# Moving the split of the normalised tokens into two bf16 halves from VectorE to GpSimd, in a layer kernel on eight cores

## The reference

```python
x = L0_attn_x                       # (8, 2048, 1024)
xn = _layernorm(x, axis=-1)         # (x - mean) / sqrt(var + 1e-5)
x = x + _L0_attn_ref(xn, ...) + _L0_ffn_ref(xn, ...)

# attention: holo_linear(x, basis, phase, amp):
resonance = jnp.einsum('bli,hi->blh', x, basis)     # 1024 -> 32
w = amp * jnp.cos(phase)
return jnp.einsum('blh,oh->blo', resonance, w)      # 32 -> 1024
# ffn:
logits = x.astype(jnp.float32) @ gate_w.astype(jnp.float32).T
topk_w, topk_i = jax.lax.top_k(softmax(logits), 2)
g = silu(einsum('td,edf->etf', x, w_gate)) * einsum('td,edf->etf', x, w_up)
expert_out = einsum('etf,efd->etd', g, w_down)
```

## Time and profile before

| what | value |
|---|---|
| time, median of 2 runs | 3964.53 us (3963.12 to 3965.94) |
| the profiled execution | 3961.37 us |
| its span, first to last instruction | 3959.8 us |
| spans of the 8 cores | 3954.5 to 3959.8 us |
| mean granted TensorE clock | 0.923 on the profiled core |

### The profile page before, as it was taken

How to read it: one execution, slowest core, us unless ns; L and a number is a source line. 1 busy time by engine, 2 the same in 40 slices (tenths; PEclk the granted TensorE clock), 3 DMA queues, 4 the chain that set the end, 5 groups by cost and what they waited for, 6 DMA issues and landing times.

```text
span 3959.8 us, 45402 instructions; the slowest of 8 cores (3954.5 to 3959.8 us)
## 1 busy us (share of the span) xinstructions
PE 3079.4 (78%) x13795; PEld 1211.7 (31%) x13795; DVE 1821.3 (46%) x2660; ACT 870.2 (22%) x945; POOL 267.5 (7%) x351
## 2 busy tenths in 40 slices
PE   2444355555554489999999999999999999999996
PEld 1111011111111034343443333434334343344432
DVE  4444534444444444444444555544444455433344
ACT  0222166666664011111111100111111110011100
POOL 1000000000000101100000000111000000011000
PEclk9755599999998599999999999999999999999995
DMA  1000000000000143343333333334433333334205
GB/s 30 27 27 17 0 0 1 1 1 1 1 1 11 19 46 38 37 48 39 33 33 33 33 33 33 35 36 48 44 33 33 33 33 33 33 39 48 27 1 160
DMA packets 254434, 116.01 MB, mean 29 GB/s; under 512 B 233592, under 2 KB 233592, under 8 KB 254208
## 3 DMA queue, kind: packets, MB, share of 16 engines
q0 software_dynamic: 245248, 87.87, 21.5%
q1 hardware_dynamic: 8960, 25.24, 2.1%
HBM read 191.40 MB, written 8.39 MB: 50 GB/s over the span
## 4 chain that ended last, share of the span: by engine, by line
PE 67%; ACT 14%; DVE 10%; issue 6%; DMA 2%; DVEq 1%; POOL 0%; ACTq 0%; SPq 0%; POOLq 0%
PE p_xg L817 20%; PE p_xu L826 19%; PE p_d L859 19%; ACT pTs L636 13%; PE p_st L625 4%; PE p_t L411 2%; DVE acc L867 1%; DMA out<-o 1%; PE p_pj L295 1%; DVE gbuf L841 1%; DVE acc L718 1%; DVE o_heads L680 1%; PE p_a L606 1%; DMA wdbuf<-w_down 1%; DVE o L910 1%
## 5 line engine op out<-in xcount | busy, mean ns | idle before, releaser
L859 PE MATMUL p_d<-gbuf,wdbuf 128*128 128x512 bf16 x3520 | 836.3, 377 | 63.3 <-DVE acc L867 35.1
L817 PE MATMUL p_xg<-xnh_fm,wgbuf 128*128 128x512 bf16 x3520 | 843.7, 383 | 25.7 <-DMA wdbuf<-w_down 25.7
L826 PE MATMUL p_xu<-xnh_fm,wubuf 128*128 128x512 bf16 x3520 | 833.8, 380 | 0.0
L841 DVE TENSOR_TENSOR gbuf<-sgt,p_xu 128x512 bf16<-128x512 bf16 x440 | 302.7, 688 | 978.0 <-PE p_xu L826 947.7
L836 ACT ACTIVATE sgt<-p_xg 128x512 bf16<-128x512 f32 x440 | 262.8, 597 | 2175.6 <-PE p_xg L817 1582.8
L867 DVE TENSOR_TENSOR acc<-acc,p_d 128x512 f32<-128x512 f32 x896 | 615.5, 687 | 259.4 <-PE p_d L859 244.0
L636 ACT ACTIVATE pTs<-p_st,bias 128x2048 bf16<-128x2048 f32 x256 | 503.6, 1967 | 337.7 <-PE p_st L625 328.1
L817 PEld LDWEIGHTS p_xg<-xnh_fm,wgbuf 128*128 128x128 bf16 x3520 | 346.3, 99 | 450.0 <-issue 42.1
L826 PEld LDWEIGHTS p_xu<-xnh_fm,wubuf 128*128 128x128 bf16 x3520 | 345.4, 98 | 418.7 <-issue 6.1
L859 PEld LDWEIGHTS p_d<-gbuf,wdbuf 128*128 128x128 bf16 x3520 | 284.5, 96 | 610.6 <-issue 391.2
L625 PE MATMUL p_st<-q_fm,k_fm 64*128 64x512 bf16 x1024 | 162.3, 392 | 311.6 <-ACT pTs L636 311.2
(11 more groups left out here) (200 smaller groups left out, 1024.4 us busy)
## 6 DMA issues: line engine op xcount, KB each, us to landing
wgbuf<-w_gate POOLq DMA_DIRECT2D x88, 256.0 KB, 14.0
wubuf<-w_up POOLq DMA_DIRECT2D x88, 256.0 KB, 15.0
wdbuf<-w_down POOLq DMA_DIRECT2D x88, 256.0 KB, 16.0
x_tm<-x SPq DMA_DIRECT2D x16, 512.0 KB, 3.5
x<-x SPq DMA_DIRECT2D x16, 512.0 KB, 4.5
out<-o SPq DMA_DIRECT2D x16, 512.0 KB, 5.1
wgbuf<-sw_gate POOLq DMA_DIRECT2D x22, 256.0 KB, 11.1
wubuf<-sw_up POOLq DMA_DIRECT2D x22, 256.0 KB, 11.7
```

The source lines that it names most:

```text
L817: emit("tensor", lambda te, buf=buf, loc=loc, c=c, tg=tg, pb=pg_b: te.matmul(pb[:, :], wgbuf[buf][:, loc * 1024 + c * 128: loc * 1024 + c ...
L826: emit("tensor", lambda te, buf=buf, loc=loc, c=c, tg=tg, pb=pu_b: te.matmul(pb[:, :], wubuf[buf][:, loc * 1024 + c * 128: loc * 1024 + c ...
L841: emit("vector", lambda v, gs=gslice, ss=ss, pb=pu_b: v.tensor_tensor(gs, sgt[ss][:], pb[:, :], ALU.mult), waits=[("t", t_xu), ("s", s_sil ...
L859: first=(li == 0), last=(li == len(grp) - 1): te.matmul(pb[:, :], wdbuf[buf][:, li * 1024 + dc * 128: li * 1024 + dc * 128 + 128], gbuf[bu ...
```

## The change

The cast and the subtraction that split `xn_tm` into its halves are put into POOL's list in place of DVE's. The cast waits for DVE's scaling and, as before, for the old transposes; the subtraction waits for POOL's semaphore after the cast. All 16 transposes of a tile wait for POOL's count after the subtraction. The subtraction of the mean, which writes `xn_tm`, now also waits until POOL has read the previous tile from it.

```diff
@@ -376,7 +377,7 @@
              incs=[("v", 1)])
         emit("vector", lambda v, b=b: v.tensor_single_scalar(
             xn_tm[:], x_tm[b][:], m_t[:], ALU.subtract),
-            waits=[("s", s_sq_prev)], incs=[("v", 1)])
+            waits=[("s", s_sq_prev), ("g", g_hl_prev)], incs=[("v", 1)])
...
         hb = i % 2
-        emit("vector", lambda v, hb=hb: v.tensor_copy(xnh_tm[hb][:], xn_tm[:]),
-             waits=[hilo_free[hb]], incs=[("v", 1)])
-        emit("vector", lambda v, hb=hb: v.tensor_tensor(
-            xnl_tm[hb][:], xn_tm[:], xnh_tm[hb][:], ALU.subtract), incs=[("v", 1)])
-        v_hl = cnt["v"]
+        v_xn_ready = cnt["v"]
+        emit("gpsimd", lambda g, hb=hb: g.tensor_copy(xnh_tm[hb][:], xn_tm[:]),
+             waits=[hilo_free[hb], ("v", v_xn_ready)], incs=[("g", 1)])
+        g_hi = cnt["g"]
+        emit("gpsimd", lambda g, hb=hb: g.tensor_tensor(
+            xnl_tm[hb][:], xn_tm[:], xnh_tm[hb][:], ALU.subtract),
+            waits=[("g", g_hi)], incs=[("g", 1)])
+        g_hl = cnt["g"]
...
                 emit("tensor", lambda te, src=src, c=c, ps=ps: te.transpose(
                     ps[:, 0:128], src[:, c * 128:(c + 1) * 128], ident_bf[:]),
-                    waits=t1_free[slot] + [("v", v_hl)], incs=[("t", 1)])
+                    waits=t1_free[slot] + [("g", g_hl)], incs=[("t", 1)])
...
         hilo_free[hb] = ("t", cnt["t"])
+        g_hl_prev = g_hl
```

More of the change, by code:

```diff
@@ L362, in build_nc @@
     t_xn_read = 0
+    g_hl_prev = 0
     for i in range(2):
```

## The result

| | before | after |
|---|---|---|
| median of the comparison | 3964.83 us (11 runs) | 3985.35 us (12 runs) |
| ratio, 95% interval | | 1.0061 [1.0041, 1.0081] |
| spans of the 8 cores, median of the profiled execution | 3958.3 us | 3978.6 us |
| loop stretch, median of 8 cores (lowest to highest) | 368.8 us (367.4 to 369.4) | 388.5 us (387.4 to 389.3) |

The changed kernel is slower by 20.5 us of the medians, by 0.6% of the ratio. That is clear of no change, and well within 2%.

What follows compares the result with a forecast made beforehand. One stream of work passing between engines bounds the layer-norm loop. Per tile 0.40 + 3.38 - 2.35 = +1.43 us, by 16 tiles +22.9 us, on 3964.5 gives 3988 us, 0.6% slower; range 3967 to 4020.

Steps and rivals of the forecast that it cites:

- The stream: Layer-norm loop: one stream of work passes between engines, nobody computes beside it, so POOL's pace shows in full; period 16.83 us.
- freed time: DVE in the loop: 1.92 us freed per tile, 31 us in all, worth nothing as its next instruction waits.
- The removed stretch: From the end of DVE's scaling (L398) to PE's first transpose: 2.35 us per tile goes from the path.
- The hand-overs: DVE to POOL, POOL's cast to its subtraction, POOL to PE: 0.13 + 0.13 + 0.14 = 0.40 us added per tile.
- The pair on POOL: Cast and subtraction on POOL: 3.38 us per tile, the middle of 1.92 (DVE's speed) and 4.84 (every operand a pass).
- the count of passes at the IOTA's rate: POOL's pair with the write under the reads: one pass for the cast, two for the subtraction, 1.05 + 1.96 = 3.01 us.
- The new wait: Ahead of the mean's subtraction, on POOL's last low half: met when reached, so it costs nothing.
- The clock: PE's granted clock: tiles don't feel it; a shift could touch four blocks of 24 matmuls, some 2 us, counted as zero.
- A: Rival: POOL as fast as DVE, or work slips beside it; not slower, 3962 to 3966 us; chance 0.05.
- B: Rival: POOL's element loop slower than its passes, pair 4.84 to 6.9 us; slower within 2%, 4029 us at 6 us; chance 0.09.
- C: Rival: B's mechanism with a pair from 6.9 us on; slower by over 2%, 4061 us at 8 us; chance 0.04.
- D: Rival: one-time cost of POOL's first cast or subtraction, 6 us added once, 3994 us; chance 0.82 together with the forecast.

Runs made afterwards that it cites:

- the two half changes: Changed kernel with the subtraction back on DVE: ratio to before 0.996, stretch 371.6 us; changed kernel with the cast back on DVE: ratio 1.001, stretch 383.4 us.

## Why the prediction was right

*The stream.* The prediction read from one tile's timeline that nobody computes beside the moved pair. That held: the doubled subtraction came back in full (36.3 of 36 us), and the two half changes gave their own sums (4.5 and 16.1 us without the blocks, where 5 and 15 were worked out). DVE's 29.3 us of freed time bought nothing; its idle time ahead of the low copies took them up. One reading on the way was wrong, and nothing in the sum rests on it: of the chain's lines in the earlier trace rows not only L411 lies in the loop, but also the projections' L295, with 1%.

*The removed stretch*, 2.35 us per tile, was as read.

*The hand-overs* were taken at 0.40 us and measured 0.42. The middle one, POOL waiting for itself, was an estimate of 0.13 and is 0.15.

*The pair on POOL*, the uncertain term, was taken at 3.38 us as the middle of 1.92 and 4.84, and measured 1.04 + 2.12 = 3.16. The error of 0.22 us per tile is 3.5 us of the sum. Nearer was the count of passes at the IOTA's rate that the prediction also gave, one for the cast (1.05) and two for the subtraction (1.96), 3.01. That it came near is partly luck: the rate rests on the one IOTA of 128 elements at 0.24 us, while another of that size in the kernel before, L269, took 0.42; from that one the same two counts give 1.05 + 1.77 = 2.82. The Trainium skill's figure ("GPSIMD Engine Reference", section 3.1), by its ratio to VectorE an estimate of 2.40 us for the subtraction, was 0.28 too high; half of its 4497 ns for 2048 elements is 2.25, an estimate still above the measured 2.12.

*The new wait* was counted at nothing since it is met when reached. This term failed, on a small scale: it costs 0.07 us each time, 1.1 us in all, as the kernel with a met wait alone showed in its gaps and in its loop without the blocks. It was there to be read: DVE's instruction with one wait starts 0.11 us after the one before (L402 ends at 101.79, L404 starts at 101.90), the one with two waits after 0.18 (L398 ends at 100.92, L402 starts at 101.10), both in the earlier trace rows.

*The clock.* With 3.58 - 2.35 = 1.23 and 0.07, sixteen tiles give 20.8 us, and the stretch grew by 19.7. Without the four blocks of the projections it grew by 21.3. The blocks, on the profiled core before and then in the changed kernel, from the chains in order of time (the first and the last of before are in the earlier trace rows):

```profile
229.69 7.73 PE p_pj L295 x24
...
314.99 7.75 PE p_pj L295 x24
```

```profile
149.85 7.85 PE p_pj L295 x24
...
240.86 6.73 PE p_pj L295 x24
...
330.00 6.54 PE p_pj L295 x24
...
419.08 8.05 PE p_pj L295 x24
```

Over all cores, the median of the four blocks' sum went from 30.8 to 29.1 us. The two in the middle begin at the lower clock, 0.50, and end at 1.00. On the profiled cores the rise came some 5 us after their start before (0.50 until 234 us, 0.71 in the next microsecond, then 1.00), and 2.5 to 3 us after it in the changed kernel (0.50 until 243, 0.64, 1.00), which makes them about 1.1 us shorter each. That was the 2 us that the prediction named and counted as zero. It needn't be an effect of the change: the kernel that differs from before by one met wait had 28.7 us, less than the changed one. What sets the moment of the rise no run shows.

*Rivals.* A (not slower) is excluded by the interval. B and C (POOL's element loop slower than its passes) fall with the pair at 3.16 us. (The "3 to 5 ns per element" of B don't follow from its pair of 4.84 to 6.9 us, which is 4.7 to 6.7 ns for the two operations together.) D, a one-time cost of the first call: DVE's first scaling ends at 83.82 + 0.75 = 84.57, and the first cast starts 0.16 us later, where it was 0.13 in the second tile, with no trace of 6 us:

```profile
83.82 0.75 DVE L399 TENSOR_SCALAR xn_tm<-xn_tm,rstd_t 128x1024 f32<-128x1024 f32 x1
...
84.73 1.03 POOL L404 CAST xnh_tm<-xn_tm 128x1024 bf16<-128x1024 f32 x1 [68.81 <-DVE xn_tm L399]
```

The sum was 22.9 us; 20.5 were measured by the medians. The errors are -3.5 for the pair, +0.3 for the hand-overs and +1.1 for the wait, which makes 20.8, against 21.3 measured in the loop without the blocks and 20.5 in the medians of whole times. That the total came out so near is luck in part: the pair was taken too long and the wait too cheap, and the two errors have opposite signs. The half microsecond in the loop no run explains.

## What to carry to other kernels

Before work is moved to an idle engine, look at one period of the loop by engine: if the engines take turns, the move costs the difference of the durations and of the hand-overs, and the freed engine only waits longer. What helped this loop was a looser order: to let a consumer start on the part that is ready gave 24 us, and the next tile's steps ahead of this tile's last ones another 88, with no operation on another engine. Moving paid only after that, and then by as much as the freed engine had become the bound, here 1.6 us, or 3.0 without the projections' blocks.

And where two stretches are compared over few microseconds, look first for a part in them that varies with the clock, and take it off: here the cores' spread fell from 2 us to 0.2, and an effect of 1.1 us became visible that had the wrong sign before.

## What was not expected of the hardware

A wait that is already met isn't free: on DVE each further semaphore took 0.07 us (gaps of 0.11, 0.17 to 0.18 and 0.24 us with one, two and three waits). POOL took 1.04 us for a cast and 2.12 us for a subtraction of 128x1024 with f32 and bf16 operands, where its IOTA of 1024 elements took 1.05. That fits one pass per operand read, but no run varied the length or the types. And POOL's subtraction beside DVE's reduction slowed neither (2.12 and 1.22 us).
